# Weight spectra of a 64x64 FFT convolution: two transforms with the data as stationary operand, on two row halves of TensorE

## What is computed

```python
def _L3_conv_ref(x, weights):        # weights (O=32, C=32, 64, 64)
    x_f = jnp.fft.rfft2(x)
    k_f = jnp.fft.rfft2(weights)     # the weight spectra
    out_f = jnp.einsum('bchw,ochw->bohw', x_f, k_f)
    return jnp.fft.irfft2(out_f, s=(H, W))
...
x = x + _L0_conv_ref(_gn(x), L0_conv_weights_r, L0_conv_weights_i)
x = x + _L1_conv_ref(_gn(x), L1_conv_gain)
x = x + _L2_conv_ref(_gn(x), L2_conv_weight)
x = x + _L3_conv_ref(_gn(x), L3_conv_weights)
```

## Time and profile before

| | us |
|---|---|
| median of 3 runs (1039.05 to 1041.32) | 1040.12 |
| the profiled execution | 1039.43 |
| its span, first to last instruction | 1036.6 |
| around the span | 2.8 |
| PE busy (matmul) | 863.3 (83% of the span) |
| DVE busy | 662.1 (64%) |
| ACT busy | 521.8 (50%) |
| mean granted TensorE clock, of full speed | 0.946 |

### The profile page before, as it was taken

How to read it: one execution, slowest core, us unless ns; L and a number is a source line. 1 busy time by engine, 2 the same in 40 slices (tenths; PEclk the granted TensorE clock), 3 DMA queues, 4 the chain that set the end, 5 groups by cost and what they waited for, 6 DMA issues and landing times. The chain is left out here.

```text
span 1036.6 us, 26773 instructions
## 1 busy us (share of the span) xinstructions
PE 863.3 (83%) x10199; PEld 736.4 (71%) x10199; DVE 662.1 (64%) x1208; ACT 521.8 (50%) x900; POOL 122.3 (12%) x120
## 2 busy tenths in 40 slices
PE   6999999786467965488769999994888699998998
PEld 6999999775356854366544444444778699998998
DVE  3556464675595668968968777866566788861232
ACT  2444444476444427255458999204887322235555
POOL 0000000000101004335600231100000100001110
PEclk9999999899788988889989999997999899998999
DMA  6465758383310001000000000004000346730222
GB/s 256 164 243 169 279 197 248 109 184 81 87 23 2 0 14 24 0 1 0 0 1 2 2 1 1 1 1 97 1 0 1 82 102 143 162 81 1 101 111 112
DMA packets 48004, 79.89 MB, mean 77 GB/s; under 512 B 19386, under 2 KB 37952, under 8 KB 45136
## 3 DMA queue, kind: packets, MB, share of 16 engines
q1 hardware_dynamic: 31312, 62.39, 21.6%
q10 hardware_dynamic: 16640, 16.78, 4.7%
HBM read 50.65 MB, written 27.92 MB: 76 GB/s over the span
## 5 line engine op out<-in xcount | busy, mean ns | idle before, releaser
L1599 PE MATMUL bank<-m_xp,m_kf 128*32 128x64 f32 x2048 | 116.3, 224 | 7.4 <-DVE m_xp L1567 5.4
L1599 PEld LDWEIGHTS bank<-m_xp,m_kf 128*32 128x32 f32 x2048 | 115.8, 139 | 8.0 <-issue 8.0
L1474 DVE SCALAR_TENSOR_TENSOR X<-bank,c_power,X 32x512 f32 x128 | 96.5, 754 | 36.8 <-PE bank L1424 33.2
L926 DVE TENSOR_TENSOR X<-X,bank 128x512 f32 x64 | 43.7, 682 | 92.1 <-PE bank L912 92.1
L205 DVE BATCH_NORM_STATS2 bn<-X 128x6 f32 x128 | 85.3, 685 | 2.9 <-POOL X L1214 1.6
L1615 ACT COPY xm<-bank 64x512 f32 x64 | 32.5, 585 | 95.8 <-PE bank L1599 95.8
L1380 ACT ACTIVATE c_r<-X,c_nrm 32x1024 f32 (+1 forms) x56 | 74.8, 1337 | 2.4 <-DVE c_nrm L1448 1.1
L441 DVE COPY ks_cols<-bank 128x512 f32<-128x512 f32 x64 | 42.6, 682 | 45.9 <-PE bank L407 45.9
L438 DVE COPY ks_tt<-bank 128x512 f32<-128x512 f32 x64 | 42.3, 688 | 43.9 <-PE bank L381 43.9
L355 ACT COPY ks_spec<-bank 128x512 f32<-128x512 f32 x64 | 37.4, 585 | 65.4 <-PE bank L415 31.3
L388 PE MATMUL bank<-ks_fw,ks_tt 128*128 128x128 f32 x512 | 64.6, 278 | 0.0
(11 more groups left out here) (193 smaller groups left out, 2091.6 us busy)
## 6 DMA issues: line engine op xcount, KB each, us to landing
ks_src<-in_L_conv_weights SPq DMA_DIRECT2D x32, 512.0 KB, 5.6
kf<-ks_spec ACTq DMA_DIRECT2D x16, 1024.0 KB, 8.9
m_kf<-kf SPq DMA_DIRECT2D x32, 512.0 KB, 8.1
X<-in_x SPq DMA_DIRECT2D x4, 2048.0 KB, 11.4
out_y<-X SPq DMA_DIRECT2D x16, 512.0 KB, 2.7
xf<-f_xm SPq DMA_DIRECT2D x6, 448.0 KB
l_wb<-in_L_conv_weights_r SPq DMA_DIRECT2D x4, 512.0 KB, 12.9
l_wb<-in_L_conv_weights_i SPq DMA_DIRECT2D x4, 512.0 KB, 15.1
```

Source lines behind the costliest of these rows:

```text
L926: dve.tensor_tensor(x, x, ps[4 + c % 4][:], ALU.add).then_inc(added, 1)
L1474: dve.scalar_tensor_tensor(x, of.rearrange("p (y x) -> p y x", x=HN), filt.power[at, 2:3], x, ALU.mult, ALU.add).then_inc(added, 1)
L1599: last = pe.matmul(ps[4 * half + m // 8][at:at + C, m % 8 * N:(m % 8 + 1) * N], kf[p][:, j, :, H * half + m], xp[half][:, j, m].rearrange( ...
```

## The change

The host writes the weights in another order (outside the metric): tile n of four output channels becomes [128 partitions = (output channel parity, w), 4096 = (input channel pairs 16) x (output channel pair m) x (input parity, h)], in `kernel_tiles`. With w on the partitions no transposes are needed:

- **Rows** (`transform_rows`): the stationary operand is a piece of the weights as it was loaded, 64 partitions (one half r) x 128 columns ((input parity, h) of one channel pair); the moving operand `ks_fw` is 64x64. The products of the two halves, partitions 0 to 63 and 64 to 127, alternate, and write to two different banks. A group of 16 products fills two banks; DVE copies them (2 copies of 128x512) to `ks_rows`, with (input parity, h) on the partitions. Four groups per tile.
- **Columns** (`transform_columns`): stationary is `ks_rows` 64 partitions (h of one input parity) x 128 (4 slots x 32 channels), moving is `ks_fh` 64x128, for the real part and then, accumulated, for the imaginary part. The two halves alternate again and write to two banks. 16 products per step u, four steps per tile, 8 more of 32 stationary columns (`ks_fh0`) at u = 0. ACT copies two banks per step to `ks_spec`.
- **Order**: PE does rows m = 0 of tile n, column steps 0 and 1 of tile n-1, rows m = 1 of tile n, column steps 2 and 3 of tile n-1. The loop's body holds two tiles; first and last tile stand outside of it.
- **Buffers**: `ks_rows` and `ks_spec` have two buffers each; `ks_tt` and `ks_cols` are gone.
- **Loads**: a tile is one DMA of 2 MB, 16 KB on each partition, instead of four of 512 KB with 4 KB pieces; PE waits for the whole tile. Tiles 0 and 1 are issued at once, tile n+2 once the rows of tile n are made. The next quarter of x is issued before tile n+2 of every even n.
- **Waits**: `kf_stored` is two semaphores. SP in `l0_forward_stage` waits for all `kf` stores ahead of the loads of `wb`. That wait is new. `kf`'s layout, its two DMAs per tile and `l3_mix_stage` stay.

The core of the diff:

```diff
+    out["ks_fw"] = np.tile(out["l3_fw"][0:N, 0:N].reshape(N, 2, SLOT)[:, :, sum(SLOT_AT, [])].reshape(N, N), (2, 1))
+    out["ks_fh"], out["ks_fh0"] = (np.tile(out[k].reshape(N, 2, P), (2, 1, 1)) for k in ("l3_fh", "l3_fh0"))
...
+def kernel_tiles(w):
+    w = w.reshape(C // IB, 2, 2, C // 2, 2, N, N)
+    return w.transpose(0, 4, 6, 3, 1, 2, 5).reshape(C // IB, P, PIX)
...
-        spec = pr.sb(ctx, "ks_spec", [P, SLOT // 4, 2, IB, N])
-        src = [pr.sb(ctx, f"ks_src{p}", [P, PIX]) for p in range(2)]
-        tt = [pr.sb(ctx, f"ks_tt{p}", [P, CH]) for p in range(4)]
-        cols = pr.sb(ctx, "ks_cols", [P, IB, SLOT, C])
-        fw, fh, fh0 = (pr.sb(ctx, f"ks_{n}", [P, P]) for n in ("fw", "fh", "fh0"))
+        spec = [pr.sb(ctx, f"ks_spec{p}", [P, QUADS, 2, IB, N]) for p in range(2)]
+        src = [pr.sb(ctx, f"ks_src{p}", [P, C // 2, 2, P]) for p in range(2)]
+        rows = [pr.sb(ctx, f"ks_rows{p}", [P, 2, 2 * SLOT, C]) for p in range(2)]
+        fw = pr.sb(ctx, "ks_fw", [P, N])
+        fh, fh0 = (pr.sb(ctx, f"ks_{n}", [P, 2, P]) for n in ("fh", "fh0"))
...
-                sp.sem_inc(x_loaded, START)
-                with sp.Fori(0, tiles // 2) as i:
+                def load(n, p):
+                    sp.dma_start(src[p][:].rearrange("p c m x -> p (c m x)"), pr.ins["L3_conv_weights"][n]
+                                 ).then_inc(loaded[p], 16)
+                for p in range(2):
+                    load(p, p)
+                with sp.Fori(0, Q - 1) as i:
+                    sp.dma_start(pr.X[:, i, :], x_groups[i]).then_inc(x_loaded, 16)
                     for p in range(2):
-                        sp.wait_ge(turned, START + 32 * i + 16 * p - 16)
-                        for k in range(4):
-                            at = slice(k * PIX // 4, (k + 1) * PIX // 4)
-                            sp.dma_start(src[p][:, at], w_tiles[2 * i + p][:, at]).then_inc(loaded[p][k], 16)
-                    sp.wait_ge(x_loaded, 16 * i + START)
-                    sp.dma_start(pr.X[:, i, :], x_groups[i]).then_inc(x_loaded, 16)
+                        sp.wait_ge(turned, START + 8 * i + 4 * p + 4)
+                        load(2 * i + p + 2, p)
+                sp.dma_start(pr.X[:, Q - 1, :], x_groups[Q - 1]).then_inc(x_loaded, 16)
...
+                def transform_rows(n, p, m, nth):
+                    if m == 0:
+                        pe.wait_ge(loaded[p], 16 * nth + 16)
+                    for g in range(2):
+                        pe.wait_ge(rows_read, START + 8 * n + 4 * m + 2 * g - 2)
+                        for c in range(C // 4):
+                            for r in range(2):
+                                at = slice(r * N, (r + 1) * N)
+                                last = pe.matmul(ps[2 * g + r][:, c * N:(c + 1) * N], src[p][at, C // 4 * g + c, m], fw[at],
+                                                 start=True, stop=True)
+                        last.then_inc(turned, 1)
+                def transform_columns(n, p, u):
+                    if u == 0:
+                        pe.wait_ge(rows_read, START + 8 * n + 8)
+                    pe.wait_ge(made_read, START + 4 * n + u - 1)
+                    banks = [ps[4 + 2 * (u % 2) + j] for j in range(2)]
+                    def product(f, m, j, part, slots, mats):
+                        half, at = slice(j * N, (j + 1) * N), SLOT * part + 4 * f
+                        to = (f % 2 * 2 + m) * P
+                        return pe.matmul(banks[j][0:slots * C, to:to + P],
+                                         rows[p][half, m, at:at + slots].rearrange("p s c -> p (s c)"), mats[half, part],
+                                         start=part == 0, stop=part == 1)
+                    for f in (2 * u, 2 * u + 1):
+                        for m, part, j in np.ndindex(2, 2, 2):
+                            last = product(f, m, j, part, 4, fh)
+                    if u == 0:
+                        for m, part, j in np.ndindex(2, 2, 2):
+                            last = product(0, m, j, part, 1, fh0)
+                    last.then_inc(made, 1)
+                def tile(n, p, nth):
+                    transform_rows(n, p, 0, nth)
+                    for u in (0, 1):
+                        transform_columns(n - 1, 1 - p, u)
+                    transform_rows(n, p, 1, nth)
+                    for u in (2, 3):
+                        transform_columns(n - 1, 1 - p, u)
                 pe.sem_inc(turned, START)
+                pe.sem_inc(made, START)
                 pe.wait_ge(const, 16 * 5)
+                for m in range(2):
+                    transform_rows(0, 0, m, 0)
+                with pe.Fori(0, tiles // 2 - 1) as i:
+                    tile(2 * i + 1, 1, i)
+                    tile(2 * i + 2, 0, i + 1)
+                tile(tiles - 1, 1, tiles // 2 - 1)
+                for u in range(4):
+                    transform_columns(tiles - 1, 1, u)
...
+                dve.sem_inc(rows_read, START)
                 with dve.Fori(0, tiles // 2) as i:
                     for p in range(2):
+                        n = 2 * i + p
+                        for m in range(2):
                             if p == 1:
+                                if m == 0:
+                                    dve.wait_ge(x_loaded, 16 * i + 16)
+                                for c in range(4 * m, 4 * m + 4):
+                                    pr.chunk_stats(dve, i, c, step)
+                            if m == 0:
+                                dve.wait_ge(made, START + 4 * n - 4)
+                            for g in range(2):
+                                dve.wait_ge(turned, START + 4 * n + 2 * m + g + 1)
+                                for r in range(2):
+                                    dve.tensor_copy(rows[p][:, m, :, C // 2 * g + r:C // 2 * (g + 1):2],
+                                                    ps[2 * g + r][:].rearrange("p (c n) -> p n c", n=N)
+                                                    ).then_inc(rows_read, 1)
                     pr.group_stats(dve, i, step)
...
+                        act.wait_ge(stored[p], START + 32 * i)
+                        for u in range(4):
+                            act.wait_ge(made, START + 4 * n + u + 1)
+                            for j in range(2):
+                                c = act.copy(spec[p][:, 2 * u:2 * u + 2, :, j:IB:2].rearrange("p f t m k -> p f m t k"),
+                                             ps[4 + 2 * (u % 2) + j][:].rearrange("p (f m t k) -> p f m t k", f=2, m=2, t=2))
+                            c.then_inc(made_read, 1)
+                        act.wait_ge(made_read, START + 4 * n + 4)
                         for part in range(2):
+                            act.dma_start(pr.kf[:, :, part, n, :].rearrange("s p n -> p s n"),
+                                          spec[p][:, :, part].rearrange("p s o k -> p s (o k)")).then_inc(stored[p], 16)
...
                 sp.sem_inc(moved, START)
+                for p in range(2):
+                    sp.wait_ge(pr.kf_stored[p], START + 16 * (C // IB))
                 for w in range(4):
                     for part, n in enumerate(("L0_conv_weights_r", "L0_conv_weights_i")):
...
```

More of the change, by code:

```diff
@@ L180, in __init__ @@
         self.kf = nc.dram_tensor("kf", (SLOT // 4, P, 2, C // IB, IB * N), F32, kind="Internal").ap()
-        self.kf_stored = self.sem("kf_stored")
+        self.kf_stored = [self.sem(f"kf_stored{p}") for p in range(2)]
         self.xf = nc.dram_tensor("xf", (Q, 2, C, KT, KX * 2 * IB), F32, kind="Internal").ap()
@@ L317, in _ @@
+                def tile(n, p, nth):
[5 more added lines that the diff above has]
+                        transform_columns(n - 1, 1 - p, u)
                 pe.sem_inc(turned, START)
+                pe.sem_inc(made, START)
                 pe.wait_ge(const, 16 * 5)
-                with pe.Fori(0, tiles // 2) as i:
-                    for p in range(2):
-                        forward_products(pe, pr, src[p], tt, cols, fw, fh, fh0, 32 * i + 16 * p,
-                                         turned, turned_read, made, made_read,
-                                         lambda j: pe.wait_ge(loaded[p][j // 2], 16 * i + 16))
+                for m in range(2):
+                    transform_rows(0, 0, m, 0)
@@ L432, in copy_turned @@
-def copy_turned(dve, ps, tt, cols, base, turned, turned_read, made, after=lambda s: None):
-    for j in range(NCH):
-        dve.wait_ge(turned, START + base + j + 1)
-        if j >= 4:
-            dve.wait_ge(made, base + j - 3)
-        dve.tensor_copy(tt[j % 4][:], ps[j % 4][:]).then_inc(turned_read, 1)
-    for s in range(SLOT // 4):
-        dve.wait_ge(turned, START + base + NCH + s + 1)
-        dve.tensor_copy(cols[:, :, 4 * s:4 * s + 4].rearrange("p b s c -> p s b c"),
-                        ps[s % 4][:].rearrange("p (s b c) -> p s b c", s=4, b=IB)).then_inc(turned_read, 1)
-        after(s)
@@ L446, in copy_rows @@
```

(17 more changed lines are left out.)

82 lines of the change are left out of this document (8 added, 74 removed).

## The result

The changed kernel takes **989.75 us** (median of 4 runs, 989.12 to 990.49); the kernel before, run beside it, 1040.04 us (4 runs, 1039.05 to 1041.32). The ratio is 0.9516, 95% interval 0.95 to 0.9533. The forecast was 980, its range 967 to 996: the sign and the mechanism are right, 9.75 us of the expected gain are missing. The profiled execution took 989.12 us with a span of 987.3 (before 1039.43 and 1036.6).

A forecast was written before the change was run, and what follows sets the result against it. PE was taken to bound the kernel, filling 22.8 of 23.5 us per spectra tile. 1039.4 less 62.4 gained plus 2.5 for the moved wait gave 979.5 profiled, 980 measured; range 967 to 996, inner 972 to 987 at 60%.

The forecast's parts named there:

- (a): Rival, spectra stage row products: 64 moving columns do pay, 0.057 us per pair, DMA then bounds the tile; 969 us; 8%.
- (b): Rival, spectra stage: DMA becomes the bound, 16.2 to 17 us per tile, 6 to 11 us more, 985 to 991; 17%.
- (c): Rival, spectra stage: granted clock falls; 994 us at 0.9 on average, 1036 if half in all row phases; 8%.
- The price of a pair, 0.111 us, load-bound: Spectra stage products: two passes on alternating halves cost one full pass, 0.111 us, the weight load setting the step.
- (d): Rival, spectra stage: the two row halves do not run beside each other; pair 0.222 us, tile 30.5 us, 1103 us; 4%.
- (e): Rival, spectra stage: a load does not overlap a product of its own half; tile about 25 us, about 1052 us; 1%.
- A tile of 15.4 us: Spectra stage, PE per tile: rows 7.1, columns 7.1, small products 0.9, handoffs 0.3 us, instead of 23.5 us.
- DMA, DVE and ACT fit beside it: Spectra stage, per tile: DMA 13.9 to 14.9 of 15.4 us, DVE 10.6 at most, ACT's copies and issues also covered.
- Both new buffers "cost nothing": Spectra stage: second `ks_spec` and second `ks_rows` cost nothing as long as a tile is 15 us.
- The step that failed: the start: Tile 0's rows: 7.1 us plus about 2.6 for first 5 us at half speed, done at 20.0 us.
- The first product at 10.3: Start of the kernel: PE waits for all 2 MB of tile 0, so work begins at 10.3 us instead of 8.04.
- The moved wait, 2.5 us: SP ahead of the `wb` loads: waiting for kf stores delays a chain with no slack, 2.5 us, bounds 0 and 4.

The follow-up runs named there:

- run 1: Changed kernel with seven of eight row products streaming 128 moving columns instead of 64, the matrix given twice: 980.52 us.
- run 4: Changed kernel with the eight row products of one half in a row, then those of the other, instead of alternating: 1065.86 us (one run).
- run 8: Changed kernel with each tile of weights in four DMAs of 512 KB, 4 KB pieces, instead of one of 2 MB: 988.55 us.
- Run 7: Changed kernel with one `ks_spec` buffer instead of two, so ACT waits for the store of the tile before: 1031.17 us.
- run 3: Changed kernel with both row phases of a tile first, then all four column steps, instead of in turn: 993.13 us.
- run 6: Changed kernel with SP's wait for the kf stores put behind the issue of the `wb` loads instead of ahead: 987.71 us.
- run 2: Changed kernel with 36 transposes of the identity, result unread, on PE while tile 0 is on its way: 978.54 us.
- run 11: Changed kernel with 30 warming transposes, tile 0 in two DMAs, and constants the first products don't need moved behind tile 0: 980.83 us.
- runs 5: The changed kernel once more, unaltered, as the measure for the runs of its batch: 987.44 us.

## Why the prediction came out as it did

The forecast is inside its outer range, but not inside the inner one of 972 to 987. The outer one was wide because it took in rivals (a), (b) and part of (c), none of which came in that form; that it holds the result is in part luck.

- *The price of a pair, 0.111 us, load-bound:* the price is right (0.110), and run 1 shows that the moving columns do not matter. That the load sets it is read from rows with other products. Rival (a) falls with it; so do (d) and (e), though run 4 shows that (d) would have come true in good part for the rows with the loops the other way round (0.112 a pass while one half works, 0.088 on average).
- *A tile of 15.4 us:* right, 15.48. The handoffs cost nothing (PE busy 100.00 of 100 us) and the small products 1.18 us instead of 0.9 (80 passes take 54.78 - 49.97 = 4.81 us, 64 take 3.63).
- *DMA, DVE and ACT fit beside it:* right, PE waited for none of them after the first product. DMA share 0.86, or 13.3 us a tile, below the 13.9 to 14.9 of the estimate. Rival (b) is not the case (run 8).
- *Both new buffers "cost nothing":* true, but I did not ask what one `ks_spec` would have cost. Run 7 says 43.7 us. In the earlier trace rows the wait for the store was 5.3 us in all, since a tile of 23.5 us hid its landing; with tiles of 15.5 us, and stores that take 8.9 us in the median to land and 20.7 at worst, it would have decided the result.
- **The step that failed: the start**, "plus about 2.6 because its first 5 us run at half speed as now". Half speed cost 11.2 us, not 2.6: the first 5 us are a property of the old products, full-size passes, with which the clock was up 5.5 us after the first. Row products with 64 moving columns did not bring it up in 20.5 us (run 3: not in 27). I had the question in rival (c), but asked it of the tiles in the middle, where the answer is 1.00, and not of the start, where nothing had brought the clock up yet. That is 8.6 us.
- *The first product at 10.3:* it came at 12.50 here, 11.3 to 12.4 in the other runs without transposes. The last packet of tile 0 moved at 10.80; I had left out the time from the last packet to the release of PE, 1.7 us here and about 1 in the trace before (7.0 to 8.04). With the transfer itself slightly slower, 2.2 us.
- *The end:* the last columns took 8.5 us instead of 8.0, and 7 tiles at 0.08 over make 0.6: 1.1 us. With 8.6 and 2.2 that is 11.9 of the 12.1 us by which the stage ended late (147.90 against 135.8). The tail was 0.5 instead of 0.6, so the statistics began 12.0 us late.
- *The moved wait, 2.5 us:* not there (run 6). "That chain has no slack" was wrong: SP waited 14.3 us for POOL ahead of the first store of `xf` in the trace before, which is the case for which the forecast had named the bound 0. The sign I had given for that came: ACT's waits on `xf` are 6.65 and 6.32 us, against 6.69.
- *The sum:* by the times of the two profiled executions 50.3 us were gained, 50.4 of them up to the statistics, so the rest took 0.1 more. (The spans say 1.1; 2.8 us lay around the span before and 1.8 after.) That makes 12.0 - 2.5 + 0.1 = 9.6 us over the forecast of 979.5 for the profiled execution, as measured.

Rival (c) had about this time (994 for a clock of 0.9 on average over the stage), but by a mechanism spread over all tiles; here the products ran at half speed until 36 us, and the granted clock was 1.00 from there to the end of the stage. Why a stream of 64 columns fails to bring the clock up, yet kept it for the 10.8 us of rows in run 2 and lost it in run 11 after 9.4 us with a short wait in them, I can't say: no run varied that by itself.

## What to carry to other kernels

With 128 stationary columns in fp32 a moving operand of 64 columns saved no time against one of 128, while two row halves in alternation gave two passes for 0.110 us, the price of one full-size pass; passes on one half alone cost 0.112 each. Read the clock at the start of a kernel from the step of the passes, and not from the clock column. Price the first tiles on their own: ask which instructions will bring the clock up, and if the new ones are thinner than the old, warm PE while the first data is on its way. When a stage gets shorter, ask of each buffer what its store's landing was hidden under; here the second output buffer held 43.7 of the 52.4 us gained (runs 5 and 7).

## What the runs showed of the hardware that I had not expected

- Row products with 64 moving columns left PE busy for 20.5 us at half speed (27 us in run 3), while the same products with 128 moving columns reached full speed during their first 13.85 us, at the same number of instructions.
- Transposes alone brought the clock up: it rose at 8.0 us, 3 us after the first of them (run 2).
- The trace's record of the clock begins with its first rise; until then the stretches show 1.00, though the passes step at half speed.
- The clock can fall while PE is never idle: 0.77 on average when eight products in a row used one half of the array (run 4).
- An fp32 pass with 128 stationary columns on one half, behind another on the same half, took 0.112 us (run 4), a pair on alternating halves 0.110, with 64 moving columns as with 128 (run 1).
- On the full array, eight passes took 0.98 us with 128 stationary columns and 0.99 with 32: the loads were hidden behind the products.
- A store of 1 MB took 4.5 to 20.7 us to land while loads shared the DMA engines, with a median of 8.9; the DMA share reached 1.02 over a whole tile at 380 GB/s.
